# Turning x outside the matrix engine: VectorE block transposes and a road through HBM in place of TensorE transposes

## The reference

```python
proj = hidden_states @ in_proj_w.T          # gate, hBC, dt
hBC = silu(causal_conv4(hBC) + conv_b)
x, Bm, Cm = split(hBC)                      # x: (b, l, 128 heads, 64)
dt = softplus(dt + dt_bias)
x_dt = x * dt[..., None]
M = (Cm @ Bm.T) * exp(segment_sum(A * dt))  # per head, within a chunk
Y_diag = M @ x_dt                           # and a second term across chunks
y = Y_diag + Y_off + D * x
y = rmsnorm(y) * norm_w * silu(gate)
out = y @ out_proj_w.T
```

## Time and profile before

| | |
|---|---|
| median of 3 runs | 1680.49 us |
| the profiled execution's own time | 1681.44 us |
| its span, from the first to the last instruction | 1679.7 us |
| mean granted TensorE clock | 0.997 |
| PE, PEld busy | 1643.6 us (98%), 1356.5 us (81%) |
| DVE, ACT, POOL busy | 1244.7 us (74%), 1286.2 us (77%), 779.2 us (46%) |
| DMA moved | 166.61 MB, 30.9% of 16 engines' span |

### The profile page before, as it was taken

One profiled execution on the slowest core, in us unless ns is written; L12 is line 12 of the kernel. 1 busy time (PEld: TensorE's weight loads), 2 busy tenths in 40 slices (PEclk: granted clock), 3 DMA queues, 4 the chain that ended last, 5 costly groups with the idle time before them and its releaser, 6 DMA issues.

```text
span 1679.7 us, 27176 instructions
## 1 busy us (share of the span) xinstructions
PE 1643.6 (98%) x9464; PEld 1356.5 (81%) x9464; DVE 1244.7 (74%) x1975; ACT 1286.2 (77%) x2218; POOL 779.2 (46%) x806
## 2 busy tenths in 40 slices
PE   6999999999999999999999999999999999999998
PEld 4888777888888888888888888888888888888876
DVE  5887886777677767677767776776767777767886
ACT  4444559878888788869887788878887889689862
POOL 3565124454445355534544354444454545355470
PEclk9999999999999999999999999999999999999999
DMA  5320343233333323323323232323233333223421
GB/s 172 117 89 1 113 145 113 94 95 92 112 93 107 97 82 122 103 74 97 116 88 116 88 116 88 106 79 113 91 107 97 108 96 114 71 89 109 117 91 51
DMA packets 98662, 166.61 MB, mean 99 GB/s; under 512 B 11648, under 2 KB 49920, under 8 KB 96864
## 3 DMA queue, kind: packets, MB, share of 16 engines
q1 hardware_dynamic: 98528, 164.88, 30.9%
HBM read 158.56 MB, written 6.29 MB: 98 GB/s over the span
## 4 chain that ended last, share of the span: by engine, by line
PE 80%; DVE 5%; ACT 2%; issue 1%; POOL 1%; DVEq 0%; POOLq 0%; ACTq 0%
PE bank L156 15%; PE bank L158 15%; PE bank L157 14%; PE bank L2217 7%; PE bank L2251 7%; PE bank L2252 7%; PE bank L2255 7%; PE bank L2239 3%; PE bank L2203 3%; PE bank L2305 1%; ACT m_mt L1582 1%; DVE m_xc L1882 1%; DVE m_y L1961 1%; DVE m_y L1951 0%; DVE m_gate L1882 0%
## 5 line engine op out<-in xcount | busy, mean ns | idle before, releaser
L156 PE MATMUL bank<-xh,w_h 128*128 128x512 f32 x1152 | 469.1, 407 | 6.2 <-DVE m_xc L1882 3.7
L158 PE MATMUL bank<-xh,w_l 128*128 128x512 f32 x1152 | 452.6, 393 | 0.0
L157 PE MATMUL bank<-xl,w_h 128*128 128x512 f32 x1152 | 449.8, 390 | 0.0
L1489 POOL TENSOR_TENSOR m_z_l<-m_zg,m_z_h 128x512 fp32r<-128x512 f32 x128 | 188.1, 1469 | 472.9 <-ACT m_z_h L1636 472.9
L1582 ACT ACTIVATE m_mt<-m_mt,m_unit 128x128 f32<-128x128 f32 x1024 | 312.3, 390 | 0.0
L1471 POOL TENSOR_TENSOR w_l<-w_raw,w_h 128x512 fp32r<-128x512 f32 x142 | 184.8, 1302 | 265.2 <-ACT w_h L1549 265.2
L156 PEld LDWEIGHTS bank<-xh,w_h 128*128 128x128 f32 x1152 | 217.0, 188 | 57.5 <-issue 17.1
L158 PEld LDWEIGHTS bank<-xh,w_l 128*128 128x128 f32 x1152 | 216.6, 188 | 48.0
L1882 DVE SCALAR_TENSOR_TENSOR m_xc<-bank,m_par_conv,m_xc 128x1020 f32<-128x1020 f32 (+2 forms) x192 | 244.3, 1273 | 14.6 <-ACT m_xc L1561 10.1
L157 PEld LDWEIGHTS bank<-xl,w_h 128*128 128x128 f32 x1152 | 217.2, 189 | 39.7
L1893 DVE TENSOR_TENSOR x<-x,bank 128x512 f32<-128x512 f32 x128 | 87.7, 685 | 202.9 <-PE bank L2255 202.8
(11 more groups left out here) (315 smaller groups left out, 2871.4 us busy)
## 6 DMA issues: line engine op xcount, KB each, us to landing
m_mt<-ncs_rows SPq DMA_DIRECT2D x128, 512.0 KB, 4.5
w_raw<-w_in SPq DMA_DIRECT2D x144, 256.0 KB, 2.9
m_wo_raw<-w_out_in SPq DMA_DIRECT2D x64, 256.0 KB, 3.7
m_e<-ecs_rows SPq DMA_DIRECT2D x128, 128.0 KB, 3.5
a_wo_raw<-wo_in SPq DMA_DIRECT2D x8, 1024.0 KB, 4.9
x<-x_in SPq DMA_DIRECT2D x8, 256.0 KB, 5.1
a_wq_raw<-wq_in SPq DMA_DIRECT2D x8, 256.0 KB, 3.2
x_saved<-x SPq DMA_DIRECT2D x1, 2048.0 KB, 7.9
```

Of the source, the lines that this page charges most:

```text
L156: nc.tensor.matmul(out, ah, bh, start=first, stop=False)
L157: nc.tensor.matmul(out, ah, bl, start=False, stop=False)
L158: return nc.tensor.matmul(out, al, bh, start=False, stop=last)
L1489: nc.gpsimd.tensor_tensor(z_l[:, s % 2, :, :], zg[:], f(z_h[:, s % 2, :, :]), ALU.subtract).then_inc(zl_ready, 1)
```

## The change

Between two steps the turned x now takes another way, for 120 of the 128 tiles of x. VectorE transposes x in blocks of 32x32 within its partitions into `x_blocks` (`turn_blocks`, two a pair of steps, both in the odd step); SyncE writes `x_blocks` to a buffer in HBM (`write_x`, one DMA of 256 KB) and reads it back with the blocks in their places into `x_rows` (`read_x`, four DMAs of 64 KB in runs of 512 bytes); GpSimd scales from `x_rows` into `xdt` in two instructions of 128x256 (`times_dt`). `x_blocks` and `x_rows` are single buffers. The 8 tiles of the last group's second half are still turned by TensorE (`turned_by_tensor`). `to_chunk_end` moves from the end of GpSimd's odd step to the start of its even step. The convolution's and the norm's parameters are no longer loaded at once and copied by VectorE (16 small copies), but loaded by group into two slots.

```diff
+    def turned_in(kind, s):
+
+        return [s + 1, s + 2] if s % 2 == 1 and ahead(kind, s + 1) and not turned_by_tensor(kind, s) else []
+
+    def turned_by_tensor(kind, s):
+
+        return [s + 1] if kind == "last" and NT - 1 <= s < STEPS - 1 else []
+
+    def scaled_first(kind, s):
+
+        return [s] if s % 2 == 0 and own(kind) and paired(kind, s) else []
+
+    def scaled_last(kind, s):
+
+        return [s + 1] if s % 2 == 0 and own(kind) and paired(kind, s) else []
...
+    def nth(g, s):
+
+        return g * STEPS + s
...
-    def conv_par(m):
+    def group_of(g, m):
+
+        return g + m // TILES + (1 if m % TILES >= LEAD else 0)
...
+    def dn_par(g, i):
+
+        return par_slots[:, g % 2, CONV_PAR + i:CONV_PAR + i + 1]
...
+            def load_par(g):
+                sp.wait_ge(conv_done, conv_at(g - 2, LEAD - 3))
+                sp.wait_ge(y_ready, at(g - 1, -1))
+                sp.dma_start(par_slots[:, g % 2, :], par[:, g, :]).then_inc(par_loaded, 16)
+
+            def write_x(g, s):
+                g, s = normal(g, s)
+                i = nth(g, s)
+                sp.wait_ge(x_turned, i + 1)
+                sp.dma_start(xt_dram[i % XT_BUFS], x_blocks[:].rearrange("p j c e -> p j (c e)")
+                             ).then_inc(x_written[i % 2], 16)
+
+            def read_x(g, s):
+                g, s = normal(g, s)
+                i = nth(g, s)
+                sp.wait_ge(x_written[i % 2], 16 * (i // 2 + 1))
+                sp.wait_ge(xdt_ready, at(g, s - 1))
+                blocks = xt_dram[i % XT_BUFS].rearrange("(a r) j c -> j r a c", a=BLOCKS)
+                for j in range(BLOCKS):
+                    sp.dma_start(x_rows[j * BLOCK:(j + 1) * BLOCK, :].rearrange("r (a c) -> r a c", a=BLOCKS),
+                                 blocks[j]).then_inc(x_landed[i % 2], 16)
...
+                for made in scaled_last(kind, s):
+                    read_x(g, made)
...
+                if kind == "middle" and s == 2:
+                    load_par(g + 1)
+                for made in turned_in(kind, s)[:1]:
+                    write_x(g, made)
...
+                for made in turned_in(kind, s)[:1]:
+                    read_x(g, made)
...
+                for made in turned_in(kind, s)[1:]:
+                    write_x(g, made)
...
+            def times_dt(g, s):
+                half, t = divmod(s, NT)
+                i = nth(g, s)
+                pool.wait_ge(unit_loaded[half], (g + 1) * 16)
+                pool.wait_ge(x_landed[i % 2], 64 * (i // 2 + 1))
+                pool.wait_ge(diag_done, at(g, s - 2))
+                if s % 2 == 0:
+                    pool.wait_ge(xdd_ready, pair(g, s - 2))
+                if i < 2:
+                    pool.wait_ge(n.turned, NT)
+                for side in range(2):
+                    last = nc.gpsimd.tensor_tensor(heads_of(xdt[:, s % 2, :], side), side_of(x_rows, side),
+                                                   side_spread(unit[:, half, t * UH:(t + 1) * UH], side), ALU.mult)
+                last.then_inc(xdt_ready, 1)
...
             def step(g, s, kind):
+                for made in scaled_first(kind, s):
+                    times_dt(g, made)
+                if s % 2 == 0 and own(kind):
+                    to_chunk_end(g, s)
                 for m in EARLY[s]:
                     if has_tile(kind, m) and has_tile(kind, m + 2):
                         w_low(g, m + 2)
+                for made in scaled_last(kind, s):
+                    times_dt(g, made)
...
-                if s % 2 == 1 and ahead(kind, s + 1):
-                    to_chunk_end(g, s + 1)
...
+            def turn_blocks(g, s):
+                g, s = normal(g, s)
+                half, t = divmod(s, NT)
+                i = nth(g, s)
+                if t == 0:
+                    dve.wait_ge(silu_done, conv_at(g - 1 + half, X_LAST[half]))
+                if i >= 1:
+                    dve.wait_ge(x_written[(i - 1) % 2], 16 * ((i - 1) // 2 + 1))
+                nc.vector.transpose(x_blocks[:], xc[:, half, :, t * P:(t + 1) * P].rearrange(
+                    "p c (j e) -> p j c e", e=BLOCK)).then_inc(x_turned, 1)
...
+                for made in turned_in(kind, s)[:1]:
+                    turn_blocks(g, made)
                 if behind(kind, s - 2):
...
-                if ahead(kind, s + 1) and s != STEPS - 1:
-                    times_dt(g, s + 1)
+                for made in turned_in(kind, s)[1:]:
+                    turn_blocks(g, made)
+                for made in turned_by_tensor(kind, s):
+                    times_dt_from_bank(g, made)
...
-                last.then_inc(x_turned, 1)
+                last.then_inc(last_turned, 1)
...
-                if ahead(kind, s + 1) and s != STEPS - 1:
-                    turn(g, s + 1)
+                for made in turned_by_tensor(kind, s):
+                    turn(g, made)
...
-                if s == STEPS - 1 and kind != "last":
-                    pe.wait_ge(cb_across_ready, g + 2)
-                    turn(g, s + 1)
```

More of the change, by code:

```diff
@@ L42 @@
 LEAD = 8
+BLOCK = 32
+BLOCKS = P // BLOCK
+XT_BUFS = 4
 W_BUFS, WO_BUFS, ROW_BUFS = 3, CT, 4
@@ L91, in mixer_kernel @@
             ssm_block(nc, inner, sems, cleared, w_sems, ssm_norm, x_saved, ident, bank, x, xh, xl, xdt, w_bufs, w_in, w_dt, par, dt_bias,
-                      a_log, w_out, ncs_dram, ecs_dram, units_dram, ffn1, out)
+                      a_log, w_out, ncs_dram, ecs_dram, units_dram, xt_dram, ffn1, out)
 class Norm:
@@ L986, in ssm_block @@
 def ssm_block(nc, ctx, sems, cleared, w_sems, n, x_saved, ident, bank, acc, xh, xl, xdt, w_bufs, w_in, w_dt, par, dt_bias, a_log, w_out,
-              ncs_dram, ecs_dram, units_dram, ffn, out):
+              ncs_dram, ecs_dram, units_dram, xt_dram, ffn, out):
     def sb(name, shape, dt=F32):
@@ L1028, in ssm_block @@
     wo_l = sb("wo_l", [P, CT, DIM], F32R)
+    x_blocks = sb("x_blocks", [P, BLOCKS, CT, BLOCK])
+    x_rows = sb("x_rows", [P, XW])
     ncs_units = ncs_dram.rearrange("t (g u h) s -> g u t h s", g=SG, u=2)
@@ L1144, in ssm_block @@
     x_turned = sem("x_turned")
+    last_turned = sem("last_turned")
+    x_written = [sem(f"x_written{i}") for i in range(2)]
+    x_landed = [sem(f"x_landed{i}") for i in range(2)]
     xdt_ready = sem("xdt_ready")
@@ L1290, in place, with conv_par, side_of, heads_of @@
         return xc[:, half, j, :] if j < CT else gate[:, half, j - CT, :]
-    def conv_par(m):
+    def group_of(g, m):
+        return g + m // TILES + (1 if m % TILES >= LEAD else 0)
+    def conv_par(g, m, i):
         j = ORDER[m % TILES]
-        return (j if j < 2 + CT else j - CT) * (TAPS + 1)
+        w = (j if j < 2 + CT else j - CT) * (TAPS + 1) + i
+        return par_slots[:, group_of(g, m) % 2, w:w + 1]
+    def dn_par(g, i):
+        return par_slots[:, g % 2, CONV_PAR + i:CONV_PAR + i + 1]
     def both(m):
         return bank[:, 2 * (m % 2):2 * (m % 2) + 2, :]
+    def side_of(rows, side):
+        return rows[:, side * XW // 2:(side + 1) * XW // 2].rearrange("p (a c e) -> p a c e", a=2, c=CT)
+    def heads_of(channels, side):
+        return channels.rearrange("p (c i a e) -> p i a c e", c=CT, i=2, a=2)[:, side]
+    def side_spread(values, side):
+        of_side = values.rearrange("p (c i) -> p i c", i=2)[:, side, :]
+        return of_side.unsqueeze(1).unsqueeze(3).to_broadcast([P, 2, CT, BLOCK])
     def spread(values):
@@ L1336, in _ @@
             sp.dma_start(dt_raw, w_dt.rearrange("p k h -> p (k h)")).then_inc(dt_loaded, 16)
-            for counted in (clamped, decay_ready, mt_ready, x_turned, xdt_ready, diag_done, y_ready, sq_ready,
+            for counted in (clamped, decay_ready, mt_ready, xdt_ready, diag_done, y_ready, sq_ready,
                             sq_summed, z_ready, zh_ready, zl_ready, out_done, acc_added):
@@ L1391, in _ @@
             sp.dma_start(alog[:], a_log).then_inc(bias_loaded, 16)
-            sp.dma_start(par_all[:], par).then_inc(par_loaded, 16)
+            sp.dma_start(par_slots[:, 0, :], par[:, 0, :]).then_inc(par_loaded, 16)
+            sp.dma_start(par_slots[:, 1, :], par[:, 1, :]).then_inc(par_loaded, 16)
             sp.dma_start(x_saved, acc[:]).then_inc(x_stored, 16)
@@ L1880, in taps @@
                 for back in range(1, TAPS):
-                    w = conv_par(m) + TAPS - 1 - back
                     ins = nc.vector.scalar_tensor_tensor(
-                        out=dst[:, :, back:], in0=src[:, :, 0:length - back], scalar=par_conv[:, w:w + 1],
+                        out=dst[:, :, back:], in0=src[:, :, 0:length - back], scalar=conv_par(g, m, TAPS - 1 - back),
                         in1=dst[:, :, back:], op0=ALU.mult, op1=ALU.add)
@@ L1951, in make_y @@
                     last = nc.vector.scalar_tensor_tensor(
-                        out=y[:, ct, :], in0=xc[:, half, ct, t * P:(t + 1) * P], scalar=par_dn[:, d:d + 1],
```

(13 more changed lines are left out.)

38 lines of the change are left out of this document (14 added, 24 removed).

## The result

The changed kernel takes 1651.14 us (median, 1648.68 to 1652.54) beside 1680.57 for the kernel before: a ratio of 0.9826, 95% interval [0.9809, 0.9844], 29.4 us less. The profiled execution has a span of 1650.8 us.

A forecast was written before the change was run, and what follows sets the result against it. TensorE, busy 98% of the span, was taken as the bound. From the profiled 1681.44 us, - 51.0 + 15.6 + 3.1 + 1 gave 1650.1, stated as 1650, with a range of 1632 to 1684.

The forecast's parts named there:

- The turns, -51.0: TensorE's transposes of x: 116 turns count as saved at 0.44 us each, 51.0 us less.
- The series ahead of `m_z_l`, +15.6: GpSimd, even steps: TensorE waits for `m_z_l` 1.04 us in step 4, 0.52 in steps 8 and 12; 15.6 us.
- L: Even steps: time from the end of xdt(s) until x(s + 1) has landed, taken as 4.4 us (3.2 to 5.3).
- X: Even steps: start of GpSimd's block to the end of `m_z_l`, 8.3 us; each further microsecond costs 29 us.
- D: GpSimd: time of one `times_dt`, taken as 1.3 us, between 1.1 and 1.8.
- The port rival: GpSimd's products stretched by 0.93 us beside VectorE's SBUF reads: 1664 to 1677 us, chance 0.12.
- Step 14, +3.1: TensorE waits for VectorE's y of step 13, so step 14's saved turn is lost: 7 x 0.44 = 3.1 us.
- ScalarE in steps 3 and 4, rival at 0.04: ScalarE, with 19.59 us of work, bounds the pair falling to 19.56: about 1670 us, chance 0.04.
- VectorE at nothing: VectorE swaps 120 products of 0.68 us for 120 block transposes taken at 0.68: no cost, given 47 us idle a group.
- The start, +1: Start of group 0: x(0) and x(1) arrive later before the head products, mostly hidden by ScalarE: 1 us, 0 to 3.5.
- Parameters, SyncE, DMA: Parameter loads by group and SyncE's added issues cost nothing; DMA engines go from 31% busy to perhaps 45%.
- The slower rival: The read of x lands late, at L of 6 us: 1697 us, even at L = 5.5; chance 0.14.

The follow-up runs named there:

- e9: Changed kernel with blocks and rows of x in one two-buffer ring, four squares a group on VectorE, GpSimd's order `m_z_l`, `times_dt`, sums: 1626.26 us.
- e10: Changed kernel with blocks and rows of x in one two-buffer ring, GpSimd's order `m_z_l`, `times_dt`, sums, all squares on ScalarE: 1638.05 us.
- the ring: Changed kernel with turned blocks and landed rows in one ring of two buffers, so the read of x(s + 1) no longer waits for xdt(s): 1650.27 us.
- e4: Changed kernel with each tile of x read by eight DMAs of 32 KB in place of four of 64 KB: 1691.5 us.
- the squares on the kernel before: Kernel before the change with four of a group's sixteen squares of y on VectorE in place of ScalarE: 1680.29 us.

## Why the prediction came out right, and where its steps did not

The time was forecast as 1650 and is 1651.14. The mechanism named, GpSimd's series ahead of `m_z_l`, is there; but one bound was costed at nothing, the turns and two of the series' parts were mis-sized, and these errors cancel. So the closeness is in part luck.

Where the time goes can be read from start to start, with e9 as the measure, since TensorE is its only bound. Worked out from TensorE's starts in both traces, groups 1 to 6, the changed kernel is late by 1.9 us a group at `m_z_l` (steps 4, 8, 12 and 0), by 0.9 at `m_z_h` (steps 4 and 13) and by 0.2 at y in step 14, together nearly all of the 3.2 between the two columns. Times 7 groups, as an estimate, that is 13, 6.5 and 1 us.

- **The turns, -51.0.** Somewhat small. The chain's 0.44 us a turn is 0.485 in undisturbed pairs, and 116 x 0.485 = 56. No run got that whole; with the later bounds out of the way (e9) the kernel is 52.8 us faster.
- **The series ahead of `m_z_l`, +15.6.** Right in kind and nearly in size. Taking both of its causes away (e10) is worth 13.1 us against the changed kernel, 11.6 against its own before. The waits shown before `m_z_l` are only 8.7 - 0.8 = 7.9 of it, because of the 0.16 us that each hides; from start to start `m_z_l`'s first product is late by 13.9 us in sum over 128 steps, 1.7 before the change, and its four take 1.20 us in place of 1.07 when late. The slope was 24 us for each us of L and 34 for each us of X, not 29.
- **D and L.** L is 3.44 to 3.6 us in most steps, at times up to 4.95, not 4.4: the read waits for four issues (1.75 us together) and lands quickly. D is 1.20 alone (1.3 was taken), but the second `times_dt` took 2.0 to 2.25 beside the mask in most groups of steps 0 and 8 and in half of those of step 4. The two errors cancelled, by luck: X was 8.28 in step 0 and 7.96 in step 4. The port rival was there in small, inside the forecast X, not on top of it. The places were not quite the forecast ones either. `m_z_l`'s product came late by 0.67 us in step 4, 0.32 in step 8 and 0.23 in step 12 in the mean, where 1.04, 0.52 and 0.52 were forecast, and by 0.45 in step 0, where I had none.
- **Step 14, +3.1.** The wait was there, 1.2 us in sum, but as a term it was mis-sized: from start to start it grew by 0.1 us a group, 0.7 in all. The pair loses more than that, for another reason: steps 13 to 15 stand 0.66 above e9's in the changed kernel and 1.18 in e10. The cause lies one step earlier, in step 13, where ScalarE's `m_z_h` is late (0.30 at 753.81, its first product 0.38 from start to start in the mean), then VectorE's addition to x, then y. e9 against e10 shows it: less work on ScalarE, and the y waits were gone.
- **ScalarE in steps 3 and 4, rival at 0.04.** This is the step that failed. I read 19.59 busy of 20.44, saw that the pair would fall to 19.56, and let it cost nothing. It costs: e10 to e9 is 11.8 us, of which the table puts some 0.37 x 7 = 2.6 in steps 3 to 5 and 1.2 x 7 = 8.3 in steps 13 to 15, which I had not looked at. The trace of the kernel before had it, with ScalarE at 21.92 of the pair's 23.08 us:

```profile
756.82:779.90 23.08, 22.94 (x141) 19.06 (x140) 19.30 (x25) 21.92 (x39) 11.14 (x12) 1.00 0.28 88
```

  That leaves 1.16 us free, and ScalarE had only one pause in this window, near its end. In step 4 ScalarE's lateness (0.72) comes first and hides part of GpSimd's (0.42 more is left), and a turn was worth more than I took, so the sum without ScalarE came close to the truth. That is luck of the balance. It is also part of why the ring alone gave nothing; the stretched products and the later y in its trace are the rest.
- **VectorE at nothing.** Nearly right: 0.70 us a transpose where 0.68 was taken, and its double costs 3.7 us. The Trainium skill's advice for turning a tile on TensorE ("VectorE: DVE Perf Modes", section "Rules for kernel authors") speaks against this change; the runs do not bear it out here, where TensorE is the bound: 29.4 us less. The prediction's estimate of 1.24 us for a block transpose is far from the 0.70 measured.
- **The start, +1.** TensorE waits 2.6 us for the second tile there, but this did not reach the time: the second head products start at 286.35, before at 264.69 + 22.76 = 287.45.
- **Parameters, SyncE, DMA.** Nothing, nothing that TensorE waits for, and 46.1% where some 45% were forecast. `m_mt` lands in 5.7 us.
- **The slower rival** was decided at L = 5.5. L = 5.21 in e4 already made the kernel slower, 1691.5: the even point lies near L = 3.5 + 29.4/24 = 4.7 by a straight line between the two runs, an estimate, so this margin was thinner than I wrote.

What stays open: the new order of e10 without the ring was not run, so the ring's own share in it is not shown; nor is how much of e10's gain over the ring is GpSimd's order alone and how much VectorE's earlier addition to x behind it; why removing the turns alone (e1) loses more in steps 5 to 7 was read from one wait (the mask), not tried by itself; and why e9 went 10 us below what was expected of it was not looked into.

## What to carry to other kernels

When one engine is busy 98% and loses work, list each stretch in which another engine fills nearly all of the new, shorter time, and price each: there were two here, and the prediction looked at one and let it cost nothing. Two engines that are late at the same place don't add up, and work moved earlier can meet other work that stretches it, so one cure can show almost nothing (0.9 us for the ring) and all together 25. Before a bound shifts, an edit can be worth zero (the squares on the kernel before) and afterwards 4 to 12 us; and in an in-order queue the order can matter as much as the length (12.2 us here with the same work): what another engine waits for goes first, what is wanted a step later next, and the sums, which are wanted latest, last.
